# Edge attributes staged slot by slot in a PSUM bank, and VectorE's turn interleaved, in a graph-network kernel

## The reference

```python
def _gine_layer(x, src, dst, edge_attr, W1l, b1l, gl, bl, W2l, b2l):   # twice
    msg = jax.nn.relu(x[src] + edge_attr)
    agg = jax.ops.segment_sum(msg, dst, num_segments=N_NODES)
    h = (x + agg) @ W1l + b1l
    ...
def _gin_conv(x, edge_index, wA, bA, wB, bB, eps):                     # twice
    agg = jax.ops.segment_sum(x[src], dst, num_segments=x.shape[0])
    h = (1.0 + eps) * x + agg
    h = jax.nn.relu(h @ wA.T + bA) @ wB.T + bB
    return h
h = jnp.maximum(_layernorm(x, axis=-1), 0.0)
x = x + _L0_gnn_ref(h, ...)
h = jnp.maximum(_layernorm(x, axis=-1), 0.0)
x = x + _L1_gnn_ref(h, ...)
```

## Time and profile before

| | |
|---|---|
| time, median of 3 runs | 2890.95 us (2886.95 to 2901.49) |
| the profiled execution: its own time | 2894.24 us |
| its span, first to last instruction | 2892.4 us |
| busy: PE / DVE / ACT / POOL | 1880.9 / 1622.1 / 530.4 / 2027.4 us |
| granted TensorE clock, mean | 0.836 of full speed |
| layer 0's gathers from the node table, first to last start | 56.13 to 1044.26 us |
| layer 1's gathers, first to last start | 1100.35 to 2122.01 us |

### The profile page before, as it was taken

How to read it: one execution, slowest core, us unless ns; L and a number is a source line. 1 busy time by engine, 2 the same in 40 slices (tenths; PEclk the granted TensorE clock), 3 DMA queues, 4 the chain that set the end, 5 groups by cost and what they waited for, 6 DMA issues and landing times.

```text
span 2892.4 us, 28711 instructions
## 1 busy us (share of the span) xinstructions
PE 1880.9 (65%) x9233; PEld 1287.9 (45%) x9233; DVE 1622.1 (56%) x2017; ACT 530.4 (18%) x618; POOL 2027.4 (70%) x2060
## 2 busy tenths in 40 slices
PE   3665556565556464565555555555557999989998
PEld 2444434443434342343434444343434566546655
DVE  7966666666666644565656666665746222352223
ACT  4111111111111122112121222222244000120001
POOL 6677777777777735777777777777724777457773
PEclk7787777777778777878787888888887999999999
DMA  6333333333333423434343444444425666466663
GB/s 192 105 115 103 122 103 115 110 121 110 119 120 122 123 75 104 132 122 137 123 149 123 143 129 149 144 140 159 137 76 168 207 219 211 131 197 218 198 201 110
DMA packets 224849, 403.63 MB, mean 140 GB/s; under 512 B 41224, under 2 KB 129116, under 8 KB 224740
## 3 DMA queue, kind: packets, MB, share of 16 engines
q1 hardware_dynamic: 159204, 267.94, 26.7%
q0 software_dynamic: 65536, 134.35, 17.2%
HBM read 337.92 MB, written 64.21 MB: 139 GB/s over the span
## 4 chain that ended last, share of the span: by engine, by line
POOL 53%; PE 25%; issue 17%; DVE 4%; DMA 1%; ACT 1%; DVEq 0%; POOLq 0%; SPq 0%; ACTq 0%
POOL xg L550 53%; PE psA L1282 17%; PE psG L1297 4%; PE psG L1346 2%; PE psA L1354 1%; PE psG L1261 0%; PE psG L1376 0%; DVE cell_room L911 0%; DVE hid L994 0%; PE psA L1363 0%; DVE xp_room L768 0%; DVE acc L844 0%; DVE hid L886 0%; DMA hid<-in_src_dram 0%; DVE xp_room L1000 0%
## 5 line engine op out<-in xcount | busy, mean ns | idle before, releaser
L550 POOL DMA_INDIRECT xg<-node_table,src_all x1536 | 1530.2, 996 | 536.9 <-issue 467.7
L1261 PE MATMUL psG<-hid,xp_room 128*128 128x160 f32 x3136 | 655.0, 387 | 764.2 <-DVE hid L886 763.0
L1261 PEld LDWEIGHTS psG<-hid,xp_room 128*128 128x128 f32 x3136 | 631.9, 264 | 807.2 <-issue 807.2
L570 POOL DMA_INDIRECT xg<-node_table,idx x480 | 461.2, 961 | 268.5 <-issue 263.5
L911 DVE TENSOR_SCALAR cell_room<-psG,cell_all 128x1960 f16<-128x1960 int16 x544 | 630.1, 1217 | 0.0
L923 DVE TENSOR_TENSOR xp_room<-xp_room,xg 128x1024 f32<-128x1024 f32 x192 | 233.3, 1216 | 639.1 <-DMA xg<-node_table,src_all 639.1
L1246 PE MATMUL psA<-cell_room,xp_room 128*128 128x512 f16 (+1 forms) x2176 | 478.4, 370 | 145.1 <-ACT count_out L618 145.1
L1246 PEld LDWEIGHTS psA<-cell_room,xp_room 128*128 128x128 f16 x2176 | 206.6, 98 | 386.4 <-ACT count_out L618 180.1
L618 ACT CAST count_out<-psA 128x1960 f16<-128x1960 f32 x96 | 172.0, 1792 | 967.0 <-PE psA L1246 967.0
L623 ACT ACTIVATE xp_room<-xp_room 128x1024 f32<-128x1024 f32 x196 | 206.1, 1057 | 672.1 <-DVE xp_room L923 667.7
L886 DVE SCALAR_TENSOR_TENSOR hid<-loc_all,round_off,psG 128x2560 f32<-128x2560 f32 x98 | 280.4, 2861 | 0.0
(11 more groups left out here) (140 smaller groups left out, 683.3 us busy)
## 6 DMA issues: line engine op xcount, KB each, us to landing
xp_room<-in_edge_attr_dram SPq DMA_DIRECT2D x98, 768.0 KB, 4.7
cell_room<-count_store SPq DMA_DIRECT2D x16, 3000.0 KB, 11.7
count_store<-count_out SPq DMA_DIRECT2D x96, 490.0 KB, 3.3
hid<-count_store SPq DMA_DIRECT2D x16, 2880.0 KB
xp_room<-in_edge_attr_dram SPq DMA_DIRECT2D x98, 256.0 KB, 5.1
xg<-node_table,src_all POOLq DMA_INDIRECT x1536, 2.5
node_table<-rows_h SPq DMA_DIRECT2D x48, 256.0 KB, 2.3
xg<-node_table,idx POOLq DMA_INDIRECT x480
```

What stands on the lines that cost most here:

```text
L550: nc.gpsimd.indirect_dma_start(xg[:, n % 2, u, j, :], None, x if n < RAW_TURNS else table, bass.IndirectOffsetOnAxis(ap=src_all[:, s, j:j ...
L570: nc.gpsimd.indirect_dma_start(xg[:, q, u, j, :], None, table, bass.IndirectOffsetOnAxis(ap=idx[:, q, u, j:j + 1], axis=0),).then_inc(row_ ...
L1261: last = nc.tensor.matmul(psG[:, q, h * WIN:(h + 1) * WIN], ea[:, t, u, j, :], hot[:, q, u, j, :], start=(u == slots[0] and j == 0), stop= ...
```

## The change

1. DVE's sum no longer adds `xg` to `ea` where both lie in SBUF. ScalarE copies one slot of `ea` (512 columns) into `ea_stage`, the fourth bank of `psG`; DVE adds the slot of `xg` to it and writes the result into `ea`. There is one staging buffer: ACT stages slot `i + 1` after DVE has summed slot `i`, and DVE waits for the staging (`ea_staged`). There are four sums of 512 columns to a turn in place of two of 1024.
2. To free that bank, `iota_bank` shrinks to 980 numbers in one bank. Each chunk's `cells` row is made by two instructions of 980 columns: the second adds 980 to the row before it compares.
3. DVE's turn is interleaved: `src_hot`, then before each slot's sum the chunks that `slot_chunks` gives it (none before slot 0, a third each before slots 1, 2 and 3).
4. ACT's evictions move from the head of the turn to behind the slot whose chunks end the unit (`units_out`).
5. Gathers are counted by slot, not by half; `summed` too; POOL's wait is for the same half as before. PE waits for each half's messages ahead of that half's products.
6. Chunks are spread over 46 turns of a layer instead of 47, and start with the third turn (before: the second). The sums of turn 2 stand at the end of DVE's turn 0, ahead of all chunk work.
7. At the start, `raw_statistics(0)` and `raw_sums(0)` stand later in DVE's order, and DVE reads the plan's numbers (`load_plan`) ahead of layer 1 and not before layer 0.

```diff
-IOTA = CB + CB % 2
+IOTA = CB // 2
...
-COUNT_TURNS = TURNS - 2
+COUNT_TURNS = TURNS - 1 - RAW_TURNS
...
-    at = [c0 + (c1 - c0) * min(max(t - 1, 0), COUNT_TURNS) // COUNT_TURNS for t in (k, k + 1)]
+    at = [c0 + (c1 - c0) * min(max(t - RAW_TURNS, 0), COUNT_TURNS) // COUNT_TURNS for t in (k, k + 1)]
...
+def slot_chunks(n, u):
+
+    chunks = turn_chunks(n)
+    return [c for i, c in enumerate(chunks) if 1 + i * (SLOTS - 1) // len(chunks) == u]
+
+
+def units_in(chunks):
+
+    return [UNIT_OF[c] for c in chunks if c + 1 in UNIT_END]
...
-        iota_bank = psG[:, 2:4, :].rearrange("p k c -> p (k c)").bitcast(I16)
+        iota_bank = psG[:, 2, :].bitcast(I16)
+        ea_stage = psG[:, 3, 0:EPP * D]
...
-                            pool.wait_ge(summed, (n - 2) * WINDOWS + h + 1)
+                            pool.wait_ge(summed, (n - 2) * SLOTS + HALVES[h][-1] + 1)
...
-                            ).then_inc(gathered[n % 2][h], 16)
+                            ).then_inc(gathered[n % 2][u], 16)
...
+            def units_out(chunks):
+
+                for k in units_in(chunks):
+                    act.wait_ge(cells_used, UNIT_END[k])
+                    if k >= 2:
+                        act.wait_ge(count_stored[k % 2], 16 * (k // 2))
+                    act.copy(count_out[:, k % 2, :], psA[:, :, :].rearrange("p k c -> p (k c)")[:, 0:CB]
+                             ).then_inc(count_evicted, 1)
+
+            def stage_attributes(i):
+
+                n, u = divmod(i, SLOTS)
+                if u == 0:
+                    act.wait_ge(ea_loaded[n % RING], 32 * (n // RING + 1))
+                act.copy(ea_stage, ea[:, n % RING, u, :, :].rearrange("p j d -> p (j d)")).then_inc(ea_staged, 1)
+
+            def messages(n, slots):
+
+                half = ea[:, n % RING, slots[0]:slots[-1] + 1, :, :].rearrange("p u j d -> p (u j d)")
+                act.activation(half, half, ACT.Relu).then_inc(msg_ready, 1)
+
             def edges(layer):
-                for n in range(layer * TURNS, (layer + 1) * TURNS):
-                    t = n % RING
-                    for k in turn_units(n):
-                        act.wait_ge(cells_used, UNIT_END[k])
-                        if k >= 2:
-                            act.wait_ge(count_stored[k % 2], 16 * (k // 2))
-                        act.copy(count_out[:, k % 2, :], psA[:, :, :].rearrange("p k c -> p (k c)")[:, 0:CB]
-                                 ).then_inc(count_evicted, 1)
-                    for h, slots in enumerate(HALVES):
-                        half = ea[:, t, slots[0]:slots[-1] + 1, :, :].rearrange("p u j d -> p (u j d)")
-                        act.wait_ge(summed, n * WINDOWS + h + 1)
-                        act.activation(half, half, ACT.Relu).then_inc(msg_ready, 1)
+                start = RAW_TURNS if layer == 0 else layer * TURNS
+                for n in range(layer * TURNS, start):
+                    for slots in HALVES:
+                        act.wait_ge(summed, n * SLOTS + slots[-1] + 1)
+                        messages(n, slots)
+                act.wait_ge(windows_cleared, 2 * (layer + 1))
+                stage_attributes(start * SLOTS)
+                for n in range(start, (layer + 1) * TURNS):
+                    for slots in HALVES:
+                        for u in slots:
+                            i = n * SLOTS + u
+                            act.wait_ge(summed, i + 1)
+                            if i + 1 < (layer + 1) * TURNS * SLOTS:
+                                stage_attributes(i + 1)
+                            if u == slots[-1]:
+                                messages(n, slots)
+                            units_out(slot_chunks(n, u))
...
+                elif hots(n) > 2:
+                    dve.wait_ge(cells_used, [c for t in range(n - RAW_TURNS) for c in turn_chunks(t)][-1] + 1)
...
-                for c in chunks:
-                    if c >= CELL_RING:
-                        dve.wait_ge(cells_used, c - CELL_RING + 1)
-                    nc.vector.tensor_scalar(cells[:, c % CELL_RING, :], iota_bank[:, 0:CB], cell_all[:, c:c + 1], None,
-                                            ALU.is_equal).then_inc(cells_ready, 1)
+
+            def chunk_cells(c):
+
+                if c >= CELL_RING:
+                    dve.wait_ge(cells_used, c - CELL_RING + 1)
+                for h in range(2):
+                    nc.vector.tensor_scalar(cells[:, c % CELL_RING, h * IOTA:(h + 1) * IOTA], iota_bank[:, 0:IOTA],
+                                            float(h * IOTA), cell_all[:, c:c + 1], ALU.add, ALU.is_equal
+                                            ).then_inc(cells_ready, 1)
+
+            def slot_sum(n, u):
+
+                dve.wait_ge(ea_staged, (n - RAW_TURNS) * SLOTS + u + 1)
+                dve.wait_ge(gathered[n % 2][u], 16 * EPP * (n // 2 + 1))
+                nc.vector.tensor_tensor(ea[:, n % RING, u, :, :].rearrange("p j d -> p (j d)"), ea_stage,
+                                        xg[:, n % 2, u, :, :].rearrange("p j d -> p (j d)"),
+                                        ALU.add).then_inc(summed, 1)
 
             def edges(layer):
                 clear_windows(layer)
                 for n in range(layer * TURNS, (layer + 1) * TURNS):
-                    count_cells(n)
-                    if n >= RAW_TURNS:
-                        dve.wait_ge(ea_loaded[n % RING], 32 * (n // RING + 1))
-                    for h, slots in enumerate(HALVES if n >= RAW_TURNS else ()):
-                        half = ea[:, n % RING, slots[0]:slots[-1] + 1, :, :].rearrange("p u j d -> p (u j d)")
-                        dve.wait_ge(gathered[n % 2][h], 16 * EPP * len(slots) * (n // 2 + 1))
-                        nc.vector.tensor_tensor(
-                            half, half, xg[:, n % 2, slots[0]:slots[-1] + 1, :, :].rearrange("p u j d -> p (u j d)"),
-                            ALU.add).then_inc(summed, 1)
-                    edge_windows(layer, n)
+                    chunk_rows(n)
+                    for u in range(SLOTS):
+                        for c in slot_chunks(n, u):
+                            chunk_cells(c)
+                        if n > RAW_TURNS:
+                            slot_sum(n, u)
+                    with dve.Fori(0, rounds) as r:
+                        windows_of(layer, n, r)
+                    if n == 0:
+                        for u in range(SLOTS):
+                            slot_sum(RAW_TURNS, u)
...
             norm_rows(0)
-            raw_statistics(0)
...
-            raw_sums(0)
+            raw_statistics(0)
...
+            raw_sums(0)
             raw_statistics(1)
...
-            skipped, pairs, use = load_plan(dve)
...
                 elif layer == 1:
+                    skipped, pairs, use = load_plan(dve)
                     dve.wait_ge(next_ready, 1 * LG)
...
-                    pe.wait_ge(cells_ready, c + 1)
+                    pe.wait_ge(cells_ready, 2 * (c + 1))
...
-                pe.wait_ge(msg_ready, (n + 1) * WINDOWS)
...
                     for h, slots in enumerate(HALVES):
+                        pe.wait_ge(msg_ready, n * WINDOWS + h + 1)
```

More of the change, by code:

```diff
@@ L115 @@
 LAYERS = 4
-RAW_TURNS = 2
-RAW_CHUNKS = SLOTS * EPP
 assert SUPERS % SLOTS == 0 and OVERLAP % EPP == 0 and SECOND <= P
 assert FIRST <= COUNTED < SUPERS and UNITS == KEPT and KEPT_TURNS % 2 == 1 and SKIP % 2 == 0
+assert CB % 2 == 0 and IOTA <= 1024 and MOST_CHUNKS <= CELL_RING and EPP * D == 512
 assert CBANKS == 4 and UPG * CW <= 512 and HALF_B * UPG >= CELL_RING * BLOCKS // 2
@@ L334, in gnn_kernel @@
         raw_step = sem("raw_step")
-        gathered = [[sem(f"gathered{q}_{h}") for h in range(WINDOWS)] for q in range(2)]
+        gathered = [[sem(f"gathered{q}_{u}") for u in range(SLOTS)] for q in range(2)]
+        ea_staged = sem("ea_staged")
         ea_loaded = [sem(f"ea_loaded{t}") for t in range(RING)]
@@ L464, in edges @@
                 for n in range(layer * TURNS, (layer + 1) * TURNS):
-                    for k in turn_units(n):
+                    for k in units_in(turn_chunks(n)):
                         sp.wait_ge(count_evicted, k + 1)
@@ L807, in raw_statistics @@
             def raw_statistics(n):
-                for h in range(WINDOWS):
-                    dve.wait_ge(gathered[n][h], 16 * EPP * len(HALVES[h]))
+                for u in range(SLOTS):
+                    dve.wait_ge(gathered[n][u], 16 * EPP)
                 for u in range(SLOTS):
@@ L838, in raw_sums @@
                             in1=ea[:, n, u, j, :], op0=ALU.mult, op1=ALU.add)
-                    if u in (HALVES[0][-1], HALVES[1][-1]):
-                        last.then_inc(summed, 1)
+                    last.then_inc(summed, 1)
             def window_add(window, first, width):
@@ L872, in add_windows, with windows_of @@
                     window_add(psG[:, q, h * WIN:(h + 1) * WIN], first, WIN).then_inc(window_added, 1)
-            def edge_windows(layer, n):
```

(30 more changed lines are left out.)

8 lines of the change are left out of this document (3 added, 5 removed).

## The result

The changed kernel takes 2804.15 us (median of 4 runs, 2802.75 to 2804.95); the kernel before took 2895.76 beside it (4 runs). The ratio of the two times is 0.9686, 95% interval 0.9656 to 0.9715. Forecast were 2799 and a range of 2787 to 2832. The profiled execution took 2802.75 us, its span is 2800.8, against 2894.2 and 2892.4 before.

What follows compares the result with a forecast made beforehand. POOL's own pace at the gathers was taken to bound both edge layers. Terms -34.4 - 44.0 - 12.6 - 1.1 = -92.1 us against 2894.2 gave 2802.1, hence 2799 (profiled execution 3.3 above median); range 2787 to 2812, with a neighbouring case 2787 to 2832.

Steps and rivals of the forecast that it cites:

- The sum from PSUM: Both edge layers: with one operand in PSUM, DVE's sum no longer holds up gathers; -34.4 and -44.0 us.
- rival D: Gathers still held by any DVE read of `xg`, 0.13 us a sum, 51 us in all, time 2850; chance 0.06.
- check by mean durations: Layers 0 and 1: gathers of 992 and 1000 ns against 945 undisturbed make 33.8 and 43.1 us lost.
- The first stall: Start of layer 0: POOL's 14.08 us wait ahead of turn 4's first gather goes; net -12.6 us.
- The tail of a layer: End of layers 0 and 1: last sum 0.69 instead of 1.22 us; -0.5 us each, -1.1 in all.
- DVE's load: DVE's turn grows from 13.60 to 14.9 us, under the 19.98 us of sixteen gathers; zero cost.
- Rival B: Half cells run one column at a time, 1.17 us each, DVE paces 92 turns: + 57, time 2856; chance 0.04.
- Staging and evictions: ACT's staging copies and evictions in each turn: longest chain stays under the gathers' 19.98 us; zero cost.
- chain of 18.8 us: From slot 3's sum through PE's windows, two chunks, eviction and copy to the next slot 3's sum; under 19.98 us.

Runs made afterwards that it cites:

- e5: The changed kernel with an extra VectorE addition of two SBUF operands, 480 columns, behind each sum: 2830.03 us.
- e6: The changed kernel with an extra VectorE addition of a PSUM and an SBUF operand, 480 columns, behind each sum: 2802.26 us.
- e1: The changed kernel with the sum reading its slot of `ea` in SBUF, not the staged copy in PSUM: 2836.64 us.
- e12: The changed kernel with all chunks of a turn ahead of slot 0 on VectorE, evictions left where they were: 2805.52 us.
- e3: The changed kernel with three half rows made for each chunk, the extra one into a spare buffer: 2803.12 us.
- e7: The changed kernel with an extra VectorE copy of one SBUF operand, 480 columns, behind each sum: 2819.78 us.
- e2: The kernel before with only chunks starting at the third turn and turn 2's sums at the end of DVE's turn 0: 2883.74 us.
- e4: The changed kernel with four half rows made for each chunk, the extra ones into a spare buffer: 2974.93 us.
- e8: The changed kernel with all chunks of a turn ahead of slot 0 and their evictions behind slot 0: 2913.11 us.
- e9: The same kernel as e12, on another chip where the kernel before took 3702.41 us: 3835.41 us.
- e11: The changed kernel with its start undone (chunks from the second turn, turn 2's sums in turn 2), where the kernel before took 3702.41 us: 3703.9 us.

## Why the prediction was right, and where it wasn't

*The sum from PSUM*: right in size, and right that the operands' place is what holds a gather. The held gathers are gone, -78.8 us of -78.4, and e5 against e6 shows the rule. But the term gave all of it to the new operand, and e1 says that about 37 us of it would have gone with the shorter sums even with both operands in SBUF. The prediction had the working for that in rival D (0.13 us a sum, measured 0.11) and didn't use it here. One slip in its check by mean durations changed nothing: 1.2486 less 0.30 is 0.949 us and not 0.945, but 0.945 is what was measured.

*The first stall*: right in kind, 2.6 us too small in this trace. The four sums with their staging ended at 93.9, not 98.1, since the one-hot build began at 86.27 (forecast for its end: 92.9, measured 89.1); either is soon enough for POOL. And `raw_sums(0)` hardly came later: it ran from 51.08 to 55.37, before from 50.72. The step "following DVE's order in its new place I get to about 57.5" failed: the part of the plan's work that now stands ahead of it began at 46.56 us, for 54.93 before, since DVE did the part ahead of that from 37.55 us on and no longer waited 3.03 us for the raw gathers first. Turn 2 began 2.1 us earlier (54.02 for 56.13), not 1.2 later, and that is in part luck. A gather beside `raw_sums(0)` is held until 56.17 us (before, until 55.83); in this trace it was turn 2's first, before it was the last raw one. With the same code turn 2 began at 53.8 and 54.2 us in e1 and e12, and between 56.3 and 56.8 in the six others, and turn 4 between 96.84 and 98.91. So the start is worth 13.2 to 15.3 us against this one trace of the kernel before, with 12.6 forecast.

*The tail of a layer*: wrong. From the last sum's start to the next window addition it is 998.45 - 997.07 = 1.38 us. In the trace before, where the sum began at 1046.83, it is 1.37 as well:

```profile
1048.20 0.32 DVE L844 TENSOR_TENSOR acc<-acc,psG 128x160 f32 x1
```

The shorter sum uncovers 0.69 us of "issue" ahead of the addition. So the term of -1.1 is 0. The stretch between the layers is 0.8 us shorter all the same, but it also varies from 53.4 to 55.7 us between kernels that share the changed code there (e1, e3, e5, e6, e7), and e2 has 54.2 with the old sums.

*DVE's load*: right, 14.4 us against 14.9 forecast, half cells 713 ns and sums 683 against 0.69 us each; the cover is over 3.7 us (e3) and under 7.4 (e4). Rival B fell with the 713 ns.

*Staging and evictions*: right for this kernel, with DVE waiting 2.1 us for ACT in all. The chain of 18.8 us itself was not measured. I had counted one eviction in a ring; e8 has two in a row behind one slot, and that turns 92 us of gain into a loss. In the changed kernel `units_out` never finds two units behind one slot, and the prediction doesn't say that its sum rests on this.

*Behind layer 1*: 3.1 us longer, not foreseen. The stretch from layer 1's last gather to the first late one was 75.6 us before and 78.5 after, and 76.5 to 78.7 in six other kernels on other chips than that of e9 to e11, with the same code there (e1, e2, e3, e5, e6, e7). e2 has the sums and cells of the kernel before and took 78.1, and e3's whole stretch from the last gather to the end is 768.8 us, shorter than before. So the change is hardly the cause, and 75.6 may be a short case. In part it is the granted clock: in 14 us that begin 17 us after layer 1's last gather it was 1.00 before with PE busy 10.8 us, and 0.88 with 12.5 us after. e6 had 1.00 and still took 78.3, so the clock isn't all of it, and the rest stays open.

## What to carry to other kernels

When an engine that only issues transfers is the bound, look at which instructions of VectorE its long ones lie under: here four additions of 512 columns with one operand in PSUM, in place of two of 1024 columns in SBUF, gave 78.8 us, though it cost ACT 226 us of copies and DVE 86 us of work that lay beside POOL's. About half of that came with the operand's place, and the other half with the shorter instructions (e1). Ask of every instruction put into an in-order queue ahead of a short, urgent one how many of its kind can stand there together: one eviction per slot was free, two in a row cost 108 us. Such a gain belongs to its bound: on a chip where PE came late, e11, which has the cheaper gathers, took as long as the kernel before.

## What was not expected of the hardware

- A copy with one SBUF operand (480 float32 columns, 426 ns) holds gathers as well: 14.8 us over 104 of them (e7). The held gather of 508.90 below ends 0.82 us after the copy, much as with the sums (0.83 before, 0.81 in e1). The hold works both ways: the copy of 503.21, begun while a gather ran, took 0.62 us, the one of 508.90 0.39.

```profile
503.21 0.62 DVE L969 COPY product<-w_first 128x480 f32<-128x480 f32 x1
...
508.90 1.21 POOL L560 DMA_INDIRECT xg<-node_table,src_all  x1 [0.30 <-issue]
508.90 0.39 DVE L969 COPY product<-w_first 128x480 f32<-128x480 f32 x1
```

- The same program took 2896 us on one chip and 3702 on another. In e11 there, gathers (948 ns) and sums (678 ns) last as long as elsewhere, and PE instructions stand 1.4 us apart with nothing waited for.
- A shorter VectorE instruction can leave the next one where it was: the window addition behind the last sum began 1.37 us after the sum's start when that took 1.23 us, and 1.38 after it when it took 0.69, with 0.69 us of "issue" between.
